# Two chained convolutions on one core: the first one split over odd and even pixels of a row, not odd and even rows

## The chip, the cores and the metric

The kernel runs on one core of a Trainium2 chip. The metric is the device time of one execution in microseconds, as the median of several executions. The five engines are called by short names below: PE (TensorE, the matrix multiplier, with PEld for its weight loads), DVE (VectorE), ACT (ScalarE), POOL (GpSimd) and SP (SyncE, which here only issues DMAs).

## What is computed

There are 8 images of 32 channels and 64 x 64 pixels, all in float32. Two blocks follow each other, each of the form "x plus a convolution of the normalised x".

```
x = x + L0(_gn(x))      # 3x3 conv, 5x5 conv, and a mix of the 5x5 result
                        # with the nine shifted 3x3 results (weights wr)
x = x + L1(_gn(x))      # for each pixel: ones and the 3x3 patch, all pairwise
                        # products of these ten, times filters (32,32,10,10)
def _gn(v, G=32, eps=1e-05):        # one group per channel: mean and variance
    m = mean over one channel's pixels; s = var over the same
    return (v - m) / sqrt(s + eps)
```

Nine shifts of a 3 x 3 convolution together with a 5 x 5 one are one 5 x 5 convolution, except at the image's border, where the shifted result was cut off. The kernel computes L0 as one 5 x 5 convolution with folded weights, plus corrections along the border.

## The kernel before

**Tiling.** Four images of 32 channels fill the 128 partitions, so there are two groups, g = 0 and 1. `raw[g]` holds x, and `plane[g]` the normalised x with a margin, at a pitch of 66 floats a row (`PITCH`). TensorE is used as 32 x 32 tiles: row group r (input partitions 32r to 32r+31) is image r, and column group s (output partitions 32s to 32s+31 of PSUM) is a "strip" s of that image. An image is worked on in two halves, h = 0 and 1 (`BANDS`). For each of them, and each image r, PSUM holds one bank `acc[:, h, r, :]` of 512 floats a partition. The upper side of the image is strips 0 and 1, the lower side strips 2 and 3, and each side gives a band of 16 rows to a half.

**Which pixels a strip is.** Before the change, of two neighbouring strips the even one holds the odd rows of the band and the odd one the even rows: 8 rows of 64 pixels, 512 outputs. A matmul with a 32 x 64 weight (two taps next to each other in y) then serves both strips from one stream of pixels, since one output row further is one tap further. `column(...)` (lines 620 to 648) walks one column of taps, `dx`, in this manner: with `pairs`, four matmuls of 32 x 64 for each image and side (`d` from -1 to 2), and without `pairs`, the two taps left over, one for each strip, as 32 x 32 matmuls on all sixteen tiles. The text calls these **pair matmuls** and **single matmuls**. Each matmul of the program is two MATMUL records in the trace. In all, the first convolution has 640 pair matmuls (1,280 records) and 320 single ones (640 records).

**Order on TensorE.** `taps0(g, h, pairs, ...)` goes over the five columns of taps in the order of `COLUMNS0`. For each group: pairs of half 0, border corrections of half 0 (`borders0`), singles of half 0, singles of half 1, border corrections of half 1, pairs of half 1. The border corrections are small matmuls: `border_row_tap` (line 655, 64 pixels of the first or last row, 20 matmuls for each g and h), `border_column_tap` (line 677, 64 pixels of the first or last column, read with a step of 66 floats, 40 for each g) and `corners` (line 665, 1 pixel). Then comes the second convolution on the same `plane`, with 13 products of shifted planes made by DVE (line 582), through the same `column`.

**Around it.** `evict` (ACT lines 327 to 334, DVE lines 542 to 549) adds nothing in the first stage and copies `acc` to `raw[g]` (a residual tap in the middle weight has already added x), image by image, three strips on ACT and strip 3 on DVE. `finish_x1` repairs borders on DVE, `statistics` and `normalise` make the next `plane[g]`. TensorE waits for a half to be evicted (`wait_evicted`) before it writes that half's banks again. There is no scheduler: every engine runs its list as written, and semaphores join them. Weights are folded on ACT and POOL (lines 363, 369, 285) and turned by a DVE transpose (line 412).

Of the kernel before, what the change touches and what calls it, by code (L numbers as in the profile page):

```python
# [5 lines left out]
B, C, H, W = 8, 32, 64, 64  # L6
GROUP = 4
NG = B // GROUP
PITCH = W + 2
# [3 lines left out]
STRIPS = 4  # L13
SIDES = 2
SIDE_ROWS = H // SIDES
BANDS = 2
BAND_ROWS = SIDE_ROWS // BANDS
CROWS = BAND_ROWS // 2
# [13 lines left out]

COLUMNS0 = (-2, -1, 1, 2, 0)
EY_EX = [(ey, ex) for ey in (-1, 0, 1) for ex in (-1, 0, 1)]
CORNERS = ((-1, -1), (-1, 1), (1, -1), (1, 1))
TAPS0 = 25
# [30 lines left out]
def conv_kernel(nc, x, w3, b3, w5, b5, wr, br, filters, out):  # L69
# [11 lines left out]
    with ctx:  # L81
# [94 lines left out]
        def product_rows(n):  # L176
            return product[n % PRODUCT_BUFS][:, PROD_AT:PROD_AT + H * PITCH]\
                .rearrange("p (y x) -> p y x", x=PITCH)[:, :, 0:W]

        def strip_rows(g, r, s, h):  # L180
# [80 lines left out]
        @block.gpsimd  # L261
        def _(pool):
            def borders_of(buf, at, length):
                nc.gpsimd.memset(buf[:, 0:at], 0.0)
                nc.gpsimd.memset(buf[:, at:at + H * PITCH].rearrange("p (y x) -> p y x", x=PITCH)[:, :, W:PITCH], 0.0)
                return nc.gpsimd.memset(buf[:, at + H * PITCH:length], 0.0)

            nc.gpsimd.memset(ones[:, :], 1.0).then_inc(zeroed, 1)
            for g in range(NG):
                borders_of(plane[g], PLANE_AT, PLANE_USED).then_inc(zeroed, 1)  # L270
            nc.gpsimd.memset(eye_from[:, :, :], 1.0).then_inc(eye_ready, 1)
            pool.wait_ge(eye_ready, 1)

            nc.gpsimd.affine_select(eye_wide[:, :, :], eye_from[:, :, :], [[-32, 4], [-1, C]], ALU.is_equal, 0.0,
                                    base=0, channel_multiplier=1).then_inc(eye_ready, 1)
            for n in range(PRODUCT_BUFS):
                borders_of(product[n], PROD_AT, PROD_USED).then_inc(borders, 1)

            pool.wait_ge(taps5_ready, 1)
            five = folded[:, 0:TAPS0, :].rearrange("p (x y) c -> p x (y c)", x=5)  # L280
            for n, (ey, ex) in enumerate(EY_EX):
                pool.wait_ge(shift_scaled, n + 1)  # L282
                three = scaled3[:, n, :, :].rearrange("p (x y) c -> p x (y c)", x=3)
                part = five[:, ex + 1:ex + 4, C * (ey + 1):C * (ey + 4)]
                nc.gpsimd.tensor_tensor(part, part, three, ALU.add).then_inc(shift_folded, 1)  # L285
                if n < len(EY_EX) - 1:
                    pool.wait_ge(shift_folded, n + 1)

        @block.scalar
        def _(act):  # L290
# [60 lines left out]
            def square(g):  # L351
# [5 lines left out]
                else:  # L357
# [2 lines left out]

            act.wait_ge(small_in, 80)
            act.wait_ge(taps5_in, 64)
            nc.scalar.activation(folded[:, 0:TAPS0, :].rearrange("p (x y) c -> p x y c", x=5),  # L363
                                 w5_in[:, :].rearrange("p (c y x) -> p x y c", y=5, x=5),
                                 ACT.Copy, scale=wr_in[:, 0:1]).then_inc(taps5_ready, 1)
            act.wait_ge(taps3_ready, 1)
            for n, (ey, ex) in enumerate(EY_EX):
# [27 lines left out]
        def _(dve):  # L395
# [6 lines left out]

            def reorder_taps():
                dve.wait_ge(small_in, 80)
                nc.vector.tensor_copy(w3_taps[:, :, :].rearrange("p (x y) c -> p x y c", x=3),  # L405
                                      w3_in[:, :].rearrange("p (c y x) -> p x y c", y=3, x=3)).then_inc(taps3_ready, 1)

            def turn_taps():

# [6 lines left out]

            def fold_edges():

                three = w3_taps[:, :, :].rearrange("p (x y) c -> p y x c", x=3)
# [117 lines left out]
            def evict(i):  # L537
# [81 lines left out]
        def _(pe):  # L619
# [29 lines left out]

            def border_row_tap(g, side, t):  # L650

                h, s, row, y = ((0, 1, 0, 0), (1, 2, CROWS - 1, H - 1))[side]
                for r in range(GROUP):
                    at = PLANE_AT + y * PITCH + t
                    nc.tensor.matmul(acc[32 * s:32 * s + 32, h, r, row * W:row * W + W],  # L655
                                     weight0[32 * r:32 * r + 32, EDGE_AT + 5 * side + t + 2, :],
                                     plane[g][32 * r:32 * r + 32, at:at + W],
                                     start=False, stop=False, tile_position=(32 * r, 32 * s))

            def corners(g, side):  # L660
                h, s, row, y = ((0, 1, 0, 0), (1, 2, CROWS - 1, H - 1))[side]
                for n, col in ((2 * side, 0), (2 * side + 1, W - 1)):
                    for r in range(GROUP):
                        at = PLANE_AT + y * PITCH + col
                        nc.tensor.matmul(acc[32 * s:32 * s + 32, h, r, row * W + col:row * W + col + 1],  # L665
                                         weight0[32 * r:32 * r + 32, CORNER_AT + n, :],
                                         plane[g][32 * r:32 * r + 32, at:at + 1],
                                         start=False, stop=False, tile_position=(32 * r, 32 * s))
# [31 lines left out]
            def wait_evicted(i):  # L700
                pe.wait_ge(evicted_act, GROUP * (i + 1))
                pe.wait_ge(evicted_dve, GROUP * (i + 1))

            def taps0(g, h, pairs, start, stop):
                for n, dx in enumerate(COLUMNS0):
                    if g == 0 and h == 0 and pairs:
                        pe.wait_ge(weight0_ready, min(n + 1, 2))
                    if dx == 0:
                        pe.wait_ge(middle_ready, g + 1)
                    five = middle0[g] if dx == 0 else weight0[:, 5 * (dx + 2):5 * (dx + 3), :]  # L710
                    last = column(h, plane[g], PLANE_AT, dx, range(-2, 3), five, start and n == 0,
                                  stop and n == len(COLUMNS0) - 1, pairs)
                return last

# [94 lines left out]
```

## Time and profile before

| | |
|---|---|
| median of 3 runs | 343.69 us (343.1 to 344.37) |
| profiled execution | 343.39 us, span 341.7 us |
| PE busy | 312.2 us, 91% of the span |
| PEld busy | 170.6 us, 50% |
| DVE busy | 180.6 us, 53% |
| ACT busy | 82.2 us, 24% |
| first MATMUL / end of the first convolution | 20.52 us / 121.3 us |

The profile is that of one execution. The span runs from its first to its last record, and the other 1.7 us of that execution's time lie around it. Records of matmuls overlap, since up to sixteen tiles work at once, so a group's mean duration is not its price: the price is read from stretches of time and the number of records in them.

### The profile page before, as it was taken

How to read it: one execution, taken by the hardware profiler on the slowest of the kernel's cores; microseconds unless marked ns; L12 is line 12 of the kernel's file. 1: busy time of each engine (PE TensorE's matmuls, PEld its weight loads, DVE VectorE, ACT ScalarE, POOL GpSimd, SP SyncE). 2: the span in 40 equal slices, each digit the busy share in tenths (PEclk: the TensorE clock that was granted, in tenths of full speed). 3: DMA queues.
4: the chain of work that ended last, by engine and by line, in shares of the span. 5: the costliest groups of instructions: out<-in, count | busy, mean ns of one | idle time of the engine just before them, and what ended most of it. 6: DMA issues, size and time to landing. Idle time of an engine off the chain costs nothing.

```text
span 341.7 us, 15524 instructions
## 1 busy us (share of the span) xinstructions
PE 312.2 (91%) x7496; PEld 170.6 (50%) x7496; DVE 180.6 (53%) x214; ACT 82.2 (24%) x135; POOL 11.3 (3%) x34
## 2 busy tenths in 40 slices
PE   0059999999999999999999999999999999999990
PEld 0023465678674445633655554744744563645550
DVE  0889628037099138205496985339003199784031
ACT  1610335052294071500000004485000000000091
POOL 3630000000000000000000000000000000000000
PEclk9999999999999999999999999999999999999998
DMA  7834100000000000000000000055000000000047
GB/s 214 279 113 107 44 4 4 2 4 3 4 4 2 4 2 3 6 2 2 4 4 2 4 4 2 17 114 125 4 2 4 2 4 2 6 2 4 4 94 154
DMA packets 7629, 11.57 MB, mean 34 GB/s; under 512 B 5392, under 2 KB 5520, under 8 KB 7440
## 3 DMA queue, kind: packets, MB, share of 16 engines
q1 hardware_dynamic: 4816, 8.54, 9.6%
q10 hardware_dynamic: 2752, 2.06, 2.2%
q8 instruction: 58, 0.95, 1.2%
q14 instruction: 3, 0.02, 0.0%
HBM read 6.40 MB, written 4.19 MB: 31 GB/s over the span
## 4 chain that ended last, share of the span: by engine, by line
PE 91%; POOL 2%; DMA 2%; issue 1%; ACTq 1%; ACT 1%; POOLq 1%; DVE 0%; DVEq 0%
PE acc L629 90%; POOL folded L285 2%; DMA w_in<-in_L_conv_w 2%; PE acc L677 1%; PE acc L655 1%; POOLq L81 1%; ACTq L236 1%; ACT folded L363 1%; DVE product L554 0%; DVEq L81 0%; PE acc L665 0%; ACTq L239 0%; ACT scaled L369 0%; DVE weight L412 0%; POOLq L282 0%
## 5 line engine op out<-in xcount | busy, mean ns | idle before, releaser
L629 PE MATMUL acc<-product,weight 32*32 32x512 f32 (+1 forms) x4416 | 182.5, 597 | 0.0
L582 DVE TENSOR_TENSOR product<-plane 128x4096 f32<-128x4096 f32 x24 | 105.1, 4424 | 63.9 <-PE acc L629 63.9
L629 PEld LDWEIGHTS acc<-product,weight 32*32 32x32 f32 (+1 forms) x4416 | 96.6, 111 | 81.8 <-issue 58.6
L629 PE MATMUL acc<-plane,weight 32*64 32x512 f32 (+1 forms) x2048 | 105.5, 603 | 21.4 <-DVE weight L412 20.5
L629 PEld LDWEIGHTS acc<-plane,weight 32*64 32x64 f32 (+1 forms) x2048 | 51.9, 121 | 65.9 <-issue 57.4
L332 ACT ACTIVATE raw<-acc,offset_by_strip 32x512 f32<-32x512 f32 x36 | 24.5, 680 | 99.5 <-PE acc L629 99.0
L629 PE MATMUL acc<-plane,middle 32*64 32x512 f32 (+1 forms) x640 | 38.2, 593 | 0.0
L330 ACT ACTIVATE raw<-acc 32x512 f32<-32x512 f32 x48 | 28.2, 588 | 36.2 <-PE acc L629 35.6
L545 DVE COPY raw<-acc 32x512 f32<-32x512 f32 x16 | 11.1, 694 | 30.9 <-PE acc L629 30.5
L629 PEld LDWEIGHTS acc<-plane,middle 32*64 32x64 f32 (+1 forms) x640 | 17.6, 119 | 12.2 <-issue 9.1
L359 ACT ACTIVATE product<-plane 128x4096 f32<-128x4096 f32 x2 | 7.3, 3636 | 63.2 <-PE acc L629 63.1
L547 DVE TENSOR_SCALAR raw<-acc,offset_by_strip 32x512 f32<-32x512 f32 x12 | 9.1, 756 | 24.0 <-PE acc L629 23.8
L500 DVE BATCH_NORM_STATS2 stats<-raw 128x6 f32<-128x512 f32 x32 | 19.5, 681 | 0.5 <-DMA raw<-in_x 0.3
L285 POOL TENSOR_TENSOR folded<-folded,scaled 128x288 f32<-128x288 f32 x9 | 8.3, 918 | 8.0 <-ACT scaled L369 7.4
L303 ACT ACTIVATE plane<-raw,norm 128x1536 f32<-128x1536 f32 x4 | 6.7, 1679 | 4.9 <-DVE norm L514 4.9
L298 ACT ACTIVATE norm<-norm 128x1 f32<-128x1 f32 x4 | 0.8, 202 | 25.5 <-DVE norm L507 25.5
L516 DVE TENSOR_SCALAR plane<-raw,mean_var,norm 128x2560 f32<-128x2560 f32 x4 | 6.8, 1712 | 0.0
L655 PE MATMUL acc<-plane,weight 32*32 32x64 f32 x160 | 5.4, 221 | 0.0
L562 DVE TENSOR_TENSOR raw<-raw,columns 128x128 f32<-128x128 f32 x2 | 0.8, 402 | 8.7 <-ACT raw L330 8.7
L655 PEld LDWEIGHTS acc<-plane,weight 32*32 32x32 f32 x160 | 4.3, 107 | 2.2 <-issue 1.8
L405 DVE COPY w_taps<-w_in 128x288 f32<-128x288 f32 x1 | 0.7, 669 | 8.8 <-DMA w_in<-in_L_conv_w 8.8
L509 DVE RECIPROCAL norm<-norm 128x1 f32<-128x1 f32 x4 | 0.7, 164 | 8.7 <-ACT norm L298 8.7
(68 smaller groups left out, 59.8 us busy)
## 6 DMA issues: line engine op xcount, KB each, us to landing
raw<-in_x SPq DMA_DIRECT2D x6, 512.0 KB, 10.2
out<-raw SPq DMA_DIRECT2D x12, 256.0 KB, 3.0
filters_in<-in_L_conv_filters SPq DMA_DIRECT2D x4, 400.0 KB, 3.9
raw<-in_x ACTq DMA_DIRECT2D x2, 512.0 KB, 8.1
out<-product SPq DMA_DIRECT2D x8, 64.0 KB, 2.4
out<-product ACTq DMA_DIRECT2D x8, 64.0 KB, 2.7
w_in<-in_L_conv_w ACTq DMA_DIRECT2D x4, 100.0 KB, 2.7
w_in<-in_L_conv_w SPq DMA_DIRECT2D x2, 36.0 KB
```

Source lines behind the costliest of these rows:

```text
L285: nc.gpsimd.tensor_tensor(part, part, three, ALU.add).then_inc(shift_folded, 1)
L303: nc.scalar.activation(inner(g, DVE_ROWS, H), raw_rows(g, DVE_ROWS, H), ACT.Identity, bias=norm[:, 6:7], scale=norm[:, 5:6]).then_inc(plan ...
L330: last = nc.scalar.activation(strip_rows(g, r, s, h), strip_acc(s, h, r), ACT.Copy)
L332: last = nc.scalar.activation(strip_rows(g, r, s, h), strip_acc(s, h, r), ACT.Identity, bias=offset_by_strip[32 * s:32 * s + 32, r, g:g + 1])
L359: nc.scalar.activation(product_rows(n), inner(g, 0, H), ACT.Square).then_inc(square_ready, 1)
L500: last = nc.vector.bn_stats(stats[:, n, :], raw[g][:, STAT * n:STAT * n + STAT])
L516: nc.vector.tensor_scalar(inner(g, 0, DVE_ROWS), raw_rows(g, 0, DVE_ROWS), mean_var[:, 0:1], norm[:, 5:6], ALU.subtract, ALU.mult).then_in ...
L545: last = nc.vector.tensor_copy(strip_rows(g, r, s, h), strip_acc(s, h, r))
L547: last = nc.vector.tensor_scalar(strip_rows(g, r, s, h), strip_acc(s, h, r), offset_by_strip[32 * s:32 * s + 32, r, g:g + 1], None, ALU.add)
L582: nc.vector.tensor_tensor(product_rows(n), inner(g, 0, H), shifted(g, PRODUCTS[k]), ALU.mult)\
L629: return nc.tensor.matmul(acc[32 * s:32 * (s + strips), h, r, :], weights[32 * r:32 * r + 32, t:t + strips, :] .rearrange("p t c -> p (t c ...
L655: nc.tensor.matmul(acc[32 * s:32 * s + 32, h, r, row * W:row * W + W], weight0[32 * r:32 * r + 32, EDGE_AT + 5 * side + t + 2, :], plane[g ...
```

## The change

The first convolution's strips become columns. Of two neighbouring strips, the even one now holds the odd pixels of each of the band's 16 rows, the odd one the even pixels: 16 rows of 32 pixels, again 512 outputs. The taps are walked row by row (`ROWS0`), and a pair of taps is two neighbours in x. A matmul's moving operand is 16 rows of 32 elements, with a step of two floats inside a row, where it was 8 rows of 64 elements with a step of one. PSUM is written as before, 512 floats in a row. The evictions of the first stage write `raw` with a step of two floats. A border row now lies on two strips, so each of its taps is two matmuls of 32 pixels. The folded weights lie in another order of taps (y outside, x inside). The second convolution, its evictions and the output stay as they are.

```diff
+        def strip_columns(g, r, s, h):
+
+            y, col = SIDE_ROWS * (s // 2) + BAND_ROWS * h, 1 - s % 2
+            return raw[g][32 * r:32 * r + 32, :].rearrange("p (y x) -> p y x", x=W)\
+                [:, y:y + BAND_ROWS, col:col + W - 1:2]
...
-            five = folded[:, 0:TAPS0, :].rearrange("p (x y) c -> p x (y c)", x=5)
+            five = folded[:, 0:TAPS0, :].rearrange("p (y x) c -> p y (x c)", y=5)
...
-                            last = nc.scalar.activation(strip_rows(g, r, s, h), strip_acc(s, h, r), ACT.Copy)
+                            last = nc.scalar.activation(strip_columns(g, r, s, h), strip_acc0(s, h, r), ACT.Copy)
...
-                            last = nc.vector.tensor_copy(strip_rows(g, r, s, h), strip_acc(s, h, r))
+                            last = nc.vector.tensor_copy(strip_columns(g, r, s, h), strip_acc0(s, h, r))
...
-                h, s, row, y = ((0, 1, 0, 0), (1, 2, CROWS - 1, H - 1))[side]
-                for r in range(GROUP):
-                    at = PLANE_AT + y * PITCH + t
-                    nc.tensor.matmul(acc[32 * s:32 * s + 32, h, r, row * W:row * W + W],
-                                     weight0[32 * r:32 * r + 32, EDGE_AT + 5 * side + t + 2, :],
-                                     plane[g][32 * r:32 * r + 32, at:at + W],
-                                     start=False, stop=False, tile_position=(32 * r, 32 * s))
+                h, half, at_row, y = ((0, 0, 0, 0), (1, 1, BAND_ROWS - 1, H - 1))[side]
+                for j in range(2):
+                    for r in range(GROUP):
+                        s = 2 * half + j
+                        at = PLANE_AT + y * PITCH + t + 1 - j
+                        nc.tensor.matmul(acc[32 * s:32 * s + 32, h, r, at_row * W // 2:(at_row + 1) * W // 2],
+                                         weight0[32 * r:32 * r + 32, EDGE_AT + 5 * side + t + 2, :],
+                                         plane[g][32 * r:32 * r + 32, at:at + W - 1:2],
+                                         start=False, stop=False, tile_position=(32 * r, 32 * s))
...
+            def tap_row(g, h, dy, weights, start, stop, pairs):
+
+
+                def tile(r, s, strips, e, t, first_one, last_one):
+                    first = PLANE_AT + (SIDE_ROWS * (s // 2) + BAND_ROWS * h + dy) * PITCH + e
+                    pixels = plane[g][32 * r:32 * r + 32, first:first + BAND_ROWS * PITCH]\
+                        .rearrange("p (y x) -> p y x", x=PITCH)[:, :, 0:W - 1:2]
+                    return nc.tensor.matmul(acc[32 * s:32 * (s + strips), h, r, :],
+                                            weights[32 * r:32 * r + 32, t:t + strips, :]
+                                            .rearrange("p t c -> p (t c)"), pixels,
+                                            start=first_one, stop=last_one, tile_position=(32 * r, 32 * s))
+
+                if pairs:
+                    for e in range(-1, 3):
+                        for s in (0, 2):
+                            for r in range(GROUP):
+                                last = tile(r, s, 2, e, e + 1, start and e == -1, stop and e == 2)
+                else:
+                    for s in range(STRIPS):
+                        for r in range(GROUP):
+                            e, t = (-2, 0) if s % 2 else (3, 4)
+                            last = tile(r, s, 1, e, t, start, stop)
+                return last
```

On TensorE, the first rows of its program before the change are these (line, operation, output and inputs, weight columns x moving elements, number of matmuls): the pairs of group 0, half 0, and its border corrections.

```order
L629 MATMUL acc<-plane,weight 64x512 x128
L629 MATMUL acc<-plane,middle_0 64x512 x32
L655 MATMUL acc<-plane,weight 32x64 x4
L677 MATMUL acc<-plane,weight 32x64 x8
L655 MATMUL acc<-plane,weight 32x64 x4
```

The same place after the change:

```order
L723 MATMUL acc<-plane,weight 64x512 x128
L723 MATMUL acc<-plane,middle_0 64x512 x32
L665 MATMUL acc<-plane,weight 32x32 x8
L689 MATMUL acc<-plane,weight 32x64 x8
L665 MATMUL acc<-plane,weight 32x32 x8
```

The large matmuls keep their number, form and place. Each group of four row taps became eight of half the length. A little further, TensorE turns from the singles of half 1 to its border corrections and its pairs. Before:

```order
L629 MATMUL acc<-plane,middle_0 32x512 x16
L655 MATMUL acc<-plane,weight 32x64 x20
L665 MATMUL acc<-plane,weight 32x1 x8
L629 MATMUL acc<-plane,weight 64x512 x128
```

After:

```order
L723 MATMUL acc<-plane,middle_0 32x512 x16
L665 MATMUL acc<-plane,weight 32x32 x40
L677 MATMUL acc<-plane,weight 32x1 x8
L723 MATMUL acc<-plane,weight 64x512 x128
```

Here the 20 row taps became 40, with nothing else between them, and nothing moved past a wait.

## Rows read from the trace of the kernel before

**Rows 1.** The page: busy time, and TensorE's granted clock in 40 slices.
```profile
PE 312.2 (91%) x7496; PEld 170.6 (50%) x7496; DVE 180.6 (53%) x214; ACT 82.2 (24%) x135; POOL 11.3 (3%) x34
...
PEclk9999999999999999999999999999999999999998
```

**Rows 2.** The chain that ended last, by line (share of the span).
```profile
PE acc L629 90%; POOL folded L285 2%; DMA w_in<-in_L_conv_w 2%; PE acc L677 1%; PE acc L655 1%; POOLq L81 1%; ACTq L236 1%; ACT folded L363 1%; DVE product L554 0%; DVEq L81 0%; PE acc L665 0%; ACTq L239 0%; ACT scaled L369 0%; DVE weight L412 0%; POOLq L282 0%
```

**Rows 3.** Waits of PE: for whom, us in total, times, longest us.
```profile
PE acc L629 <- DVE weight L412: 20.5, 1, 20.5
PE acc L629 <- issue: 0.9, 2, 0.5
```

**Rows 4.** PE by stretches: from:to, length, busy us (records), clock, DMA share, GB/s.
```profile
24.50:39.80 15.30, 15.30 (x288) 1.00 0.33 83
41.90:53.00 11.10, 10.71 (x320) 1.00 0.02 4
71.60:88.90 17.30, 17.30 (x321) 1.00 0.01 2
121.30:138.40 17.10, 17.10 (x410) 1.00 0.01 3
```

**Rows 5.** PE groups by shape: records, busy us, mean ns of one, idle before.
```profile
L629 PE MATMUL acc<-plane,weight 32*64 32x512 f32 x1280 | 73.5, 604 | 20.5 <-DVE weight L412 20.5
L655 PE MATMUL acc<-plane,weight 32*32 32x64 f32 x160 | 5.4, 221 | 0.0
L677 PE MATMUL acc<-plane,weight 32*32 32x64 f32 x160 | 4.1, 288 | 0.0
L665 PE MATMUL acc<-plane,weight 32*32 32x1 f32 x64 | 1.4, 168 | 0.0
```

**Rows 6.** The chain in order of time, 39 to 54 us: start, us, what.
```profile
39.89 0.19 PE acc L655 x4
...
41.90 1.13 PE acc L629 x20
...
53.27 0.56 PE acc L655 x35
53.83 0.13 PE acc L665 x11
```

**Rows 7.** ACT evictions of the first stage, in order of time.
```profile
48.81 7.23 ACT L330 ACTIVATE raw<-acc 32x512 f32<-32x512 f32 x12 [5.29 <-PE acc L629]
71.68 7.23 ACT L330 ACTIVATE raw<-acc 32x512 f32<-32x512 f32 x12 [15.64 <-PE acc L629]
99.45 7.21 ACT L330 ACTIVATE raw<-acc 32x512 f32<-32x512 f32 x12
121.29 7.23 ACT L330 ACTIVATE raw<-acc 32x512 f32<-32x512 f32 x12 [14.62 <-PE acc L629]
```

**Rows 8.** DVE in order of time: evictions, and the next product it waits to make.
```profile
109.15 2.86 DVE L545 COPY raw<-acc 32x512 f32<-32x512 f32 x4
121.29 2.87 DVE L545 COPY raw<-acc 32x512 f32<-32x512 f32 x4 [9.28 <-PE acc L629]
...
155.29 4.43 DVE L582 TENSOR_TENSOR product<-plane 128x4096 f32<-128x4096 f32 x1 [16.72 <-PE acc L629]
```

**Rows 9.** DVE groups by shape: border repair, columns (step 64) and rows (step 1).
```profile
L562 DVE TENSOR_TENSOR raw<-raw,columns 128x128 f32<-128x128 f32 x2 | 0.8, 402 | 8.7 <-ACT raw L330 8.7
L564 DVE TENSOR_TENSOR raw<-raw,ring_rows 128x128 f32<-128x128 f32 x2 | 0.6, 292 | 0.1
```

More of the change, by code:

```diff
@@ L31 @@
 PRODUCT_BUFS = 4
-COLUMNS0 = (-2, -1, 1, 2, 0)
+ROWS0 = (-2, -1, 1, 2, 0)
 EY_EX = [(ey, ex) for ey in (-1, 0, 1) for ex in (-1, 0, 1)]
@@ L178, in product_rows, with strip_acc0 @@
                 .rearrange("p (y x) -> p y x", x=PITCH)[:, :, 0:W]
+        def strip_columns(g, r, s, h):
+            y, col = SIDE_ROWS * (s // 2) + BAND_ROWS * h, 1 - s % 2
+            return raw[g][32 * r:32 * r + 32, :].rearrange("p (y x) -> p y x", x=W)\
+                [:, y:y + BAND_ROWS, col:col + W - 1:2]
+        def strip_acc0(s, h, r):
+            return acc[32 * s:32 * s + 32, h, r, :].rearrange("p (y x) -> p y x", x=W // 2)
         def strip_rows(g, r, s, h):
@@ L279, in _ @@
             pool.wait_ge(taps5_ready, 1)
-            five = folded[:, 0:TAPS0, :].rearrange("p (x y) c -> p x (y c)", x=5)
+            five = folded[:, 0:TAPS0, :].rearrange("p (y x) c -> p y (x c)", y=5)
             for n, (ey, ex) in enumerate(EY_EX):
                 pool.wait_ge(shift_scaled, n + 1)
-                three = scaled3[:, n, :, :].rearrange("p (x y) c -> p x (y c)", x=3)
-                part = five[:, ex + 1:ex + 4, C * (ey + 1):C * (ey + 4)]
+                three = scaled3[:, n, :, :].rearrange("p (y x) c -> p y (x c)", y=3)
+                part = five[:, ey + 1:ey + 4, C * (ex + 1):C * (ex + 4)]
                 nc.gpsimd.tensor_tensor(part, part, three, ALU.add).then_inc(shift_folded, 1)
@@ L362, in _ @@
             act.wait_ge(taps5_in, 64)
-            nc.scalar.activation(folded[:, 0:TAPS0, :].rearrange("p (x y) c -> p x y c", x=5),
-                                 w5_in[:, :].rearrange("p (c y x) -> p x y c", y=5, x=5),
+            nc.scalar.activation(folded[:, 0:TAPS0, :],
+                                 w5_in[:, :].rearrange("p (c t) -> p t c", t=25),
                                  ACT.Copy, scale=wr_in[:, 0:1]).then_inc(taps5_ready, 1)
@@ L650, in border_row_tap @@
             def border_row_tap(g, side, t):
-                h, s, row, y = ((0, 1, 0, 0), (1, 2, CROWS - 1, H - 1))[side]
-                for r in range(GROUP):
-                    at = PLANE_AT + y * PITCH + t
-                    nc.tensor.matmul(acc[32 * s:32 * s + 32, h, r, row * W:row * W + W],
-                                     weight0[32 * r:32 * r + 32, EDGE_AT + 5 * side + t + 2, :],
-                                     plane[g][32 * r:32 * r + 32, at:at + W],
-                                     start=False, stop=False, tile_position=(32 * r, 32 * s))
+                h, half, at_row, y = ((0, 0, 0, 0), (1, 1, BAND_ROWS - 1, H - 1))[side]
[7 more added lines that the diff above has]
+                                         start=False, stop=False, tile_position=(32 * r, 32 * s))
             def corners(g, side):
-                h, s, row, y = ((0, 1, 0, 0), (1, 2, CROWS - 1, H - 1))[side]
+                h, half, at_row, y = ((0, 0, 0, 0), (1, 1, BAND_ROWS - 1, H - 1))[side]
                 for n, col in ((2 * side, 0), (2 * side + 1, W - 1)):
+                    s = 2 * half + 1 - col % 2
+                    to = at_row * W // 2 + col // 2
                     for r in range(GROUP):
                         at = PLANE_AT + y * PITCH + col
-                        nc.tensor.matmul(acc[32 * s:32 * s + 32, h, r, row * W + col:row * W + col + 1],
+                        nc.tensor.matmul(acc[32 * s:32 * s + 32, h, r, to:to + 1],
                                          weight0[32 * r:32 * r + 32, CORNER_AT + n, :],
@@ L702, in wait_evicted @@
                 pe.wait_ge(evicted_dve, GROUP * (i + 1))
+            def tap_row(g, h, dy, weights, start, stop, pairs):
[18 more added lines that the diff above has]
+                return last
             def taps0(g, h, pairs, start, stop):
-                for n, dx in enumerate(COLUMNS0):
+                for n, dy in enumerate(ROWS0):
                     if g == 0 and h == 0 and pairs:
                         pe.wait_ge(weight0_ready, min(n + 1, 2))
-                    if dx == 0:
+                    if dy == 0:
                         pe.wait_ge(middle_ready, g + 1)
-                    five = middle0[g] if dx == 0 else weight0[:, 5 * (dx + 2):5 * (dx + 3), :]
-                    last = column(h, plane[g], PLANE_AT, dx, range(-2, 3), five, start and n == 0,
-                                  stop and n == len(COLUMNS0) - 1, pairs)
+                    five = middle0[g] if dy == 0 else weight0[:, 5 * (dy + 2):5 * (dy + 3), :]
+                    last = tap_row(g, h, dy, five, start and n == 0, stop and n == len(ROWS0) - 1, pairs)
                 return last
```

5 lines of the change are left out of this document (2 added, 3 removed).

## The prediction, as it was recorded before the changed kernel ran

> **What bounds the kernel now.** I read the page first. TensorE is busy for 91% of the span, at full clock in every slice but the last [rows 1]. Then the chain that ended last: 90% of it is line 629, the large matmuls of both convolutions, and the rest is mostly the start [rows 2]. Then PE's waits: it waits once for the first weights (20.5 us) and for 0.9 us besides, never for DVE, ACT or an eviction [rows 3]. So the kernel is its start plus TensorE's stream. A change in the stream's rate counts in full, a change elsewhere only if it outgrows its cover.
>
> The rate has to be read from stretches, since records overlap. A stretch of pairs has 321 records in 17.30 us [rows 4]: eight tiles (four images, two sides) run at once, so a round of 8 records takes 17.30/321 x 8 = 431 ns. A stretch of singles has 320 in 11.10 us: a round of 16 records takes 555 ns. A pair round and a single round stream as much into each tile, so the single round has some 555 - 431 = 124 ns that are not streaming. The first convolution has 1,280 pair records (160 rounds, 69 us) and 640 single ones (40 rounds, 22 us).
>
> **The change, part by part.**
>
> *The moving operand read with a step of two.* Number, length and order of the large matmuls stay. What can change is the rate of reading. The trace of before has no step of two, so I bound it from both sides. The lower bound is no cost: the output still goes to PSUM in a row and as many elements stream. The upper bound is the one stepped read there is, the border columns with a step of 66 floats [rows 5]. A 1-pixel record takes 168 ns, a 64-pixel record of neighbours 221 and of stepped pixels 288. So an element costs (221 - 168)/63 = 0.84 ns with step one and (288 - 168)/63 = 1.90 ns with step 66, that is 1.06 ns more. On 512 elements that would be 543 ns a record.
>
> Which end is nearer? Step two leaves every element's neighbour but one beside it, and every stretch of floats that is read is half used. With step 66 nothing fetched along with an element is of use. I take step two as nearer to step one, at a cost of **0**. It is the step I trust least.
>
> The Trainium skill (SBUF — State Buffer, on cachelines) says that SBUF is read in lines of 16 bytes and that two uses of a line give full bandwidth. Step two uses each line twice, so the page too would make this 0, but with nothing to spare: a row of taken pixels that starts in the second half of a line has a single use at both ends. If each such row cost one use more in 32, for half of the rows, that estimate from the page would add 1.6% to the pairs' 69 us, 1.1 us. The sum below doesn't hold it.
>
> *The border rows.* 80 matmuls of 64 pixels become 160 of 32, so 160 records are added (2 for each matmul, 40 in each of four stretches). The upper bound is today's spacing: 35 records of line 655 in 0.56 us, 16 ns each [rows 6], or 160 x 16 = 2.6 us. The lower bound is a gain: if a tile's own stream paces these stretches and not the issue, then each of its 10 records in a stretch is 32 x 0.84 = 27 ns shorter, 4 x 0.27 = 1.1 us less. Between them stands the 1-pixel row, 11 records in 0.13 us, 12 ns each [rows 6]. At 12 ns the two stretches with row taps alone go from 40 x 16 = 0.64 to 80 x 12 = 0.96 us, +0.32 each. The two that also hold column taps have 120 records between 39.89 and 41.90 us [rows 6], less 16 corner records at 12 ns, 15 ns each. There five steps of 24 records (0.36 us) would become 32 records (0.38 us), +0.1 each. I take 2 x 0.32 + 2 x 0.1 = **+0.8 us**.
>
> *The evictions.* 48 ACT and 16 DVE copies write `raw` with a step of two. Lower bound: nothing. Upper bound: DVE's repair with a step of 64 against the one with a step of one, 402 - 292 = 110 ns for 128 elements [rows 9], so 0.44 us for 512. Twelve ACT evictions of a half would take 7.23 + 5.3 = 12.5 us, DVE's four 2.87 + 1.8 = 4.6 us. Who waits? TensorE needs half 0 of group 1 emptied at 121.3 us. ACT ends it at 106.7, DVE at 112.0 [rows 7, 8], so there are 9.3 us of cover. It needs half 1 after the 384 records of half 0 of the second convolution, near 138 us (410 records lie in the 17.1 us up to 138.4 [rows 4]), and ACT ends at 128.5 us, so 10 us of cover. For group 0 the evictions end at 56.0 and 78.9 us and are needed at 71.6 and 88.9. Behind the evictions stand DVE's statistics and the next products, where DVE then idles 16.7 us [rows 8]. All cover the upper bound: **0**. If the cover were gone, each half would cost up to 5.3 us.
>
> *The weights.* Reading and folding in another order of taps keeps count, length and step of each instruction on ACT, POOL and DVE, and the first five taps are still turned first: **0** on the start of 20.5 us. The corrections' weights (line 428 and after) read with other steps, far ahead of their use at 39.8 us.
>
> The sum is made against the profiled execution, 343.39 us (span 341.7 and 1.7 around it), 0.3 below the median: 343.4 + 0 + 0.8 + 0 + 0 = 344.2 us, as a median **344.5 us**, +0.2%. This case's own range is 342.6 (borders at their gain) to 346.8 (borders at 2.6 and half a per cent on the stream).
>
> **The rivals.**
>
> *Fetches pace the stream (slower).* If a stepped read costs 1.90 ns because each element needs a fetch of its own, and a fetch with two taken elements costs the same, then step two costs 0.95 ns an element, 0.11 more than now, 56 ns a record. For it speaks that the price of a fetch, halved, is just above today's 0.84. The pairs take 160 x 56 = 9.0 us more. The singles have 124 ns a round that are not streaming, so between 0 and 2.2 us, I take 1.1. With the borders' 0.8, +10.9: **354.6 us**. It is outside 0.5% (1.7 us) from 6 ns a pair record on.
>
> *The full price of a step (slower).* Each pair record takes 543 ns more, 86.9 us. A single round goes from 555 to 431 + 543 = 974 ns, 16.8 us. With the borders: **448 us**. It needs a read that makes no use of the neighbour.
>
> *Four readers of one row group (slower).* In a single round four column groups read the same 32 partitions, in a pair round two. If the reads are shared among them and each now brings half as many useful elements, four readers at step two could be at the limit when two aren't. Then a single round takes up to 2 x 431 = 862 ns, 307 more, 40 x 307 = 12.3 us: **356.8 us**. For it: four readers at step one are the most that the trace shows. Against: nothing shows that they disturb each other now.
>
> *The gaps in the singles close (faster).* The 124 ns of a single round may come from collisions of reads: neighbouring strips now read five rows apart, and would then read the same rows, five pixels apart. If all of it goes, 40 x 124 = 5.0 us are won, **339.5 us** with the borders' 0.8. It decides from 2.5 us on, half the gaps. Against: the singles also load a weight for each record of 32 columns, twice as many in a round as the pairs, and that stays.
>
> **How the numbers follow.** The forecast has 0.44, fetches 0.27, four readers 0.09, the full price 0.07, the gaps closing 0.06, and 0.07 is for what I haven't thought of. What a measurement can tell from no change is 0.5%, 342.0 to 345.4 us. The forecast's range goes past the upper end only with the borders near their upper bound, so of its 0.44 some 0.35 are "same", 0.08 slower, 0.01 faster. Slower: 0.08 + 0.27 + 0.09 + 0.07 + 0.03 = 0.54. Faster: 0.01 + 0.06 + 0.01 = 0.08. Same: 0.38. The range takes the forecast (0.43), fetches (0.26), four readers (0.08) and a part of the rest: 342.6 to 357.2 us. It leaves out the full price and the gaps closing.
>
> **What would show it.** Pairs: the stretch of 320 records of group 1, half 0, takes 17.3 us by the forecast, 19.5 by the fetches, 39 by the full price. Singles: 320 records of group 0 take 11.1 us, by four readers up to 17.2, by closing gaps 8.6. Border stretches of half 1: near 1.0 us in place of 0.64 for the row taps. Evictions: ACT between 588 and 1,030 ns each, with no wait of PE for them. First MATMUL at 20.5 us. The prediction is wrong if step two isn't free for TensorE, and only in a small part if the borders are mis-sized.

## The result: 353.39 us, 2.8% slower

The changed kernel takes 353.39 us (median of 4 runs, 352.04 to 354.38), the kernel before 343.96 us beside it. The ratio is 1.0278, 95% interval 1.0246 to 1.0310. The profiled execution took 354.38 us, with a span of 352.6 us, 10.9 us longer than before. The medians differ by 9.4 us; the pieces below are of the two profiled executions and add up to nearly the 10.9.

The page after, with the lines that answer to [rows 1] and [rows 2]:

```profile
PE 321.0 (91%) x7656; PEld 175.6 (50%) x7656; DVE 180.8 (51%) x214; ACT 83.8 (24%) x135; POOL 11.3 (3%) x34
...
PEclk9999989999999999999999999999999999999998
...
PE acc L637 60%; PE acc L723 29%; POOL folded L294 2%; DMA w_in<-in_L_conv_w 2%; PE acc L689 1%; PE acc L665 1%; POOLq L81 1%; ACTq L245 1%; ACT folded L372 1%; DVE product L562 0%; DVEq L81 0%; PE acc L677 0%; ACTq L248 0%; ACT scaled L378 0%; DVE weight L420 0%
```

The picture is the same as before: TensorE is the chain. The 160 added records are there (7,496 became 7,656), and one slice has a lower granted clock. The waits of PE answer to [rows 3]:

```profile
PE acc L723 <- DVE weight L420: 20.7, 1, 20.7
PE acc L689 <- issue: 1.4, 1, 1.4
PE acc L677 <- issue: 1.0, 1, 1.0
PE acc L723 <- issue: 0.6, 1, 0.6
```

The start is where it was. But TensorE now stands still for 3.0 us that nothing in the profile explains ("issue"), against 0.9, and twice it does so inside the border corrections (line 689 is the column taps, 677 the corners, 665 the row taps). PE by stretches, as in [rows 4]: first singles of group 0, then its row taps of half 1, then two stretches of pairs.

```profile
45.40:58.00 12.60, 12.60 (x335) 0.86 0.01 4
58.00:59.10 1.10, 1.10 (x103) 1.00 0.00 0
59.10:77.70 18.60, 18.60 (x330) 1.00 0.01 3
77.80:96.40 18.60, 18.60 (x328) 1.00 0.01 3
```

A stretch of pairs that took 17.3 us takes 18.6 at full clock. The chain in order of time gives the best ruler, since two stretches of pairs follow each other without a break there (640 records, 80 rounds of 8). First the kernel before, then the changed one, whose other rows here are the stalls and their neighbours:

```profile
53.96 35.09 PE acc L629 x630
```

```profile
43.77 1.39 issue
...
45.42 12.59 PE acc L723 x267
58.02 1.04 PE acc L665 x53
...
59.18 37.50 PE acc L723 x604
...
100.16 0.59 issue
100.75 10.50 PE acc L723 x269
...
112.02 0.98 issue
113.25 18.89 PE acc L723 x294
132.15 33.09 PE acc L637 x714
```

A pair round went from 35.09/80 = 439 ns to 37.50/80 = 469 ns (some records are missing, the 80 rounds are the program's). Going through both chains from piece to piece, the 10.9 us lie here: four stretches of pairs +5.1 (1.5 + 2.4 + 1.2), four border stretches +3.4, singles +2.1, start +0.15. The first of the four stretches is 1.8 us longer than the last in the kernel before too (19.37 us against 17.6), which the part on the granted clock comes back to. The second convolution takes 220.4 us in both.

The evictions, as in [rows 5] and [rows 7] the group by shape and the last one in time:

```profile
L339 ACT ACTIVATE raw<-acc 32x512 f32<-32x512 f32 x48 | 30.0, 624 | 41.2 <-PE acc L723 40.5
...
L665 PE MATMUL acc<-plane,weight 32*32 32x32 f32 x320 | 6.0, 199 | 0.0
L689 PE MATMUL acc<-plane,weight 32*32 32x64 f32 x160 | 4.8, 288 | 1.4 <-issue 1.4
L677 PE MATMUL acc<-plane,weight 32*32 32x1 f32 x64 | 1.5, 172 | 1.0 <-issue 1.0
```

```profile
132.27 7.74 ACT L339 ACTIVATE raw<-acc 32x512 f32<-32x512 f32 x12 [17.23 <-PE acc L723]
```

An ACT copy went from 588 to 624 ns, and twelve from 7.23 to 7.74 us; DVE's stayed at 695 ns. No wait of PE names them.

### The profile page after: what moved, and what is told of

Same layout as the page of the kernel before. It is cut to its first block, busy times and chain, and to the rows that moved or that the text cites. A ratio compares the mean times of both kernels' runs of the same rounds, so it can differ in the third digit from the quotient of the medians.

```text
span 352.6 us, 15844 instructions
## 1 busy us (share of the span) xinstructions
PE 321.0 (91%) x7656; PEld 175.6 (50%) x7656; DVE 180.8 (51%) x214; ACT 83.8 (24%) x135; POOL 11.3 (3%) x34
## 4 chain that ended last, share of the span: by engine, by line
PE 91%; POOL 2%; DMA 2%; issue 1%; ACTq 1%; ACT 1%; POOLq 1%; DVE 0%; DVEq 0%
PE acc L637 60%; PE acc L723 29%; POOL folded L294 2%; DMA w_in<-in_L_conv_w 2%; PE acc L689 1%; PE acc L665 1%; POOLq L81 1%; ACTq L245 1%; ACT folded L372 1%; DVE product L562 0%; DVEq L81 0%; PE acc L677 0%; ACTq L248 0%; ACT scaled L378 0%; DVE weight L420 0%
## 5 line engine op out<-in xcount | busy, mean ns | idle before, releaser
L637 PEld LDWEIGHTS acc<-product,weight 32*32 32x32 f32 (+1 forms) x4416 | 98.0, 111 | 80.4 <-issue 55.6
L723 PE MATMUL acc<-plane,weight 32*64 32x512 f32 (+1 forms) x1536 | 85.5, 654 | 21.3 <-DVE weight L420 20.7
L723 PEld LDWEIGHTS acc<-plane,weight 32*64 32x64 f32 (+1 forms) x1536 | 41.8, 125 | 58.0 <-issue 55.1
L339 ACT ACTIVATE raw<-acc 32x512 f32<-32x512 f32 x48 | 30.0, 624 | 41.2 <-PE acc L723 40.5
L637 PE MATMUL acc<-plane,weight 32*64 32x512 f32 (+1 forms) x512 | 25.9, 599 | 0.0
L723 PE MATMUL acc<-plane,middle 32*64 32x512 f32 (+1 forms) x384 | 24.5, 625 | 0.0
L508 DVE BATCH_NORM_STATS2 stats<-raw 128x6 f32<-128x512 f32 x32 | 19.4, 678 | 0.1
L637 PEld LDWEIGHTS acc<-plane,weight 32*64 32x64 f32 (+1 forms) x512 | 11.6, 116 | 11.8 <-issue 9.8
L723 PEld LDWEIGHTS acc<-plane,middle 32*64 32x64 f32 (+1 forms) x384 | 11.9, 121 | 7.7 <-issue 7.0
L637 PE MATMUL acc<-plane,middle 32*64 32x512 f32 (+1 forms) x256 | 15.3, 594 | 0.0
L637 PEld LDWEIGHTS acc<-plane,middle 32*64 32x64 f32 (+1 forms) x256 | 6.5, 116 | 5.1 <-issue 3.7
L665 PEld LDWEIGHTS acc<-plane,weight 32*32 32x32 f32 x320 | 5.7, 104 | 2.3 <-issue 2.0
```

Source lines behind the costliest of these rows:

```text
L339: last = nc.scalar.activation(strip_columns(g, r, s, h), strip_acc0(s, h, r), ACT.Copy)
L508: last = nc.vector.bn_stats(stats[:, n, :], raw[g][:, STAT * n:STAT * n + STAT])
L637: return nc.tensor.matmul(acc[32 * s:32 * (s + strips), h, r, :], weights[32 * r:32 * r + 32, t:t + strips, :] .rearrange("p t c -> p (t c ...
L665: nc.tensor.matmul(acc[32 * s:32 * s + 32, h, r, at_row * W // 2:(at_row + 1) * W // 2], weight0[32 * r:32 * r + 32, EDGE_AT + 5 * side + ...
L723: return nc.tensor.matmul(acc[32 * s:32 * (s + strips), h, r, :], weights[32 * r:32 * r + 32, t:t + strips, :] .rearrange("p t c -> p (t c ...
```

## The experiments

Ratios are against the kernel before, run on the same chip. "Step" is the distance between read elements in floats.

### One part undone or done alone

**The reading undone.** In the changed kernel's `tap_row`:

```diff
-                        .rearrange("p (y x) -> p y x", x=PITCH)[:, :, 0:W - 1:2]
+                        .rearrange("p (y x) -> p y x", x=PITCH)[:, :, 0:W // 2]
```

> The changed kernel, but its large matmuls of the first convolution read 16 rows of 32 neighbouring elements in place of every other one (other pixels than the reference's, so the output differs). Theory of the step: the pairs' 18.6 us stretches go back to 17.3 and what stays is the borders' and the stalls' part, near 347.5 us in all. Rival, the form of 16 short rows and not the step: pairs stay at 18.6 us, near 353 us.

Measured: 348.56 us, ratio 1.0141 (1.0113 to 1.0169). Two stretches of pairs in the chain:

```profile
58.08 35.49 PE acc L723 x618
```

35.49 us, against 37.50 with the step and 35.09 in the kernel before. So the step costs 2.0 us of two stretches, and 16 short rows in place of 8 long ones 0.4. The form is a small part, the step the large one. The total is 1 us above what was expected for it.

**The reading alone.** In the kernel before, the large matmuls of the first convolution read what the change reads:

```diff
+                    if first_conv:
+                        first = min(first, PLANE_USED - 16 * PITCH)
+                        pixels = stack[32 * r:32 * r + 32, first:first + BAND_ROWS * PITCH]\
+                            .rearrange("p (y x) -> p y x", x=PITCH)[:, :, 0:W - 1:2]
```

> The kernel before, with nothing changed but what its large matmuls of the first convolution read: 16 rows of 32 elements with a step of two (other pixels, so the output differs). Theory of the step: the four stretches of pairs take 18.6 us in place of 17.3, 5.2 us in all, singles 0 to 1.5 us more, near 349.5 us. If the step needs the changed borders or evictions to cost something, no change from before, 344 us. If four readers of one row group hurt each other, the stretches of singles grow by several us each.

Measured: 349.96 us, ratio 1.0181 (1.0152 to 1.0210), 6.1 us more than before. The pairs again:

```profile
56.63 37.45 PE acc L633 x569
```

37.45 us, as in the changed kernel. The step needs neither the changed borders nor the evictions. Without the idle time in them, the singles of group 0 took 11.7 us against 11.0, and not several us more. Four stretches of pairs (twice 2.36 us) and the singles of two groups (1.4 us) give the 6.1.

**The added border records taken out.** In the changed kernel, `border_row_tap` issues its 20 matmuls of 64 neighbours for each half, on one strip:

```diff
-                for j in range(2):
+                for j in range(1):
                     for r in range(GROUP):
-                        s = 2 * half + j
-                        at = PLANE_AT + y * PITCH + t + 1 - j
-                        nc.tensor.matmul(acc[32 * s:32 * s + 32, h, r, at_row * W // 2:(at_row + 1) * W // 2],
+                        s = half + 1
+                        at = PLANE_AT + y * PITCH + t
+                        nc.tensor.matmul(acc[32 * s:32 * s + 32, h, r, 0:W],
...
-                                         plane[g][32 * r:32 * r + 32, at:at + W - 1:2],
+                                         plane[g][32 * r:32 * r + 32, at:at + W],
```

> The changed kernel with the border row taps in the number and form of before: 20 matmuls of 64 neighbouring elements for each half in place of 40 of 32 (on one strip alone, so the output's border rows differ). Theory: the 3.5 us that the border stretches grew, 2.0 us of them stalls with no instruction, go away, and with them the granted clock of 0.86 after the first stall: near 349.5 us. Rival, the border taps matter only by their own streaming, 0.8 us: near 352.5 us, the stalls stay.

Measured: 350.57 us, ratio 1.0201 (1.0176 to 1.0226), 2.8 us less than the changed kernel. Of PE's waits one line is left besides the start:

```profile
PE acc L723 <- issue: 0.9, 2, 0.6
```

The stalls are back at the 0.9 us of before. The expectation was 1 us too hopeful.

**The added records alone.** In the kernel before, each row tap is split into two matmuls of 32 neighbours on the same strip, and the output stays the same:

```diff
-                    nc.tensor.matmul(acc[32 * s:32 * s + 32, h, r, row * W:row * W + W],
+                    for c in (0, W // 2):
+                        nc.tensor.matmul(acc[32 * s:32 * s + 32, h, r, row * W + c:row * W + c + W // 2],
...
-                                     plane[g][32 * r:32 * r + 32, at:at + W],
+                                         plane[g][32 * r:32 * r + 32, at + c:at + c + W // 2],
```

> The kernel before with each border row tap split into two matmuls of 32 neighbouring elements, nothing else (the output stays the reference's). It has the 160 added records of the change and no stepped read. Theory: the added records cost what the changed kernel's borders and stalls did, 2.8 us by the run with wide border rows, so 346.8 us, with stalls of 1 us or more that are put down to issue in or right behind the border stretches. Rival: the stall came from the column reads or the steps, then 344.7 us at most.

Measured: 346.73 us, ratio 1.0066 (1.0050 to 1.0082), 2.5 us. The chain shows the stall in the middle of the corrections, 1.53 us long where the changed kernel has 1.39:

```profile
43.08 1.53 issue
44.92 10.41 PE acc L629 x271
55.33 1.04 PE acc L656 x54
56.57 3.59 PE acc L629 x57
```

No step is read here but the old column taps. So it is the added small matmuls that lengthen the stall, and not what they read. The row taps of half 1 (line 656) take 1.04 us, the same as line 665 after the change, and 80 records in 1.04 us are 13 ns each.

**The evictions undone.** In the changed kernel, stage 0 on ACT and DVE writes `strip_rows(g, r, s, h)` from `strip_acc(s, h, r)` again.

> The changed kernel with the first stage's evictions written as before, rows of 64 floats with a step of one (pixels go to other places, so the output differs). Theory: the evictions are covered, so ACT's copies go from 624 back to 588 ns and the time stays at 353.4 us. Rival, the writes with a step of two disturb TensorE's reads: the pairs' stretches get shorter, up to 5 us less.

Measured: 353.21 us, ratio 1.0265 (1.0227 to 1.0302). ACT's copies are back at 587 ns, the pairs take 37.41 us. The evictions' step costs nothing that can be told here and doesn't disturb TensorE's reads.

**Both costs undone.** The first and the third edit together, in the changed kernel.

> The changed kernel with both of its costs undone: the large matmuls of the first convolution read 16 rows of 32 neighbouring elements, and the border row taps have the number and form of before (other pixels and border rows than the reference's, so the output differs). What stays of the change is the 16 short rows, the evictions' step and the order of the weights. Theory: step 5.2 us and added records 2.5 to 2.8 us are all of it but some 0.2 us for each of four stretches of pairs, so 344.3 to 345.2 us. If something else in the change costs, it stays at 346 us or more.

Measured: 345.24 us, ratio 1.0033 (1.0017 to 1.0049), just above the range given. The pairs:

```profile
54.43 35.50 PE acc L723 x630
```

35.50 us is again 0.4 more than before in two stretches, 0.8 in four. That is most of the 1.2 us that are left. What the change does besides (evictions, order of the weights) has no room for a cost that can be told.

### What a stepped read costs

The next four all start from the kernel before and differ in what the first convolution's large matmuls read, in the place of the lines shown for the reading alone.

**Step four.** The rows are read as two runs of 16 elements: `[:, :, 0:W]`, then `.rearrange("p y (x j) -> p y j x", j=4)[:, :, 0:2, :]`.

> The kernel before, but the large matmuls of the first convolution read their 512 elements with a step of four floats (each of 16 rows read as two runs of 16 elements; other pixels, so the output differs). If a fetch brings four floats and costs the 1.82 to 1.9 ns of the step-66 read, each element now needs its own: 930 to 970 ns a record in place of 466 at step two, about 440 us in all. If the price is one for leaving the neighbour, whatever the step, it stays near step two, 350 us.

Measured: 435.29 us (2 runs), ratio 1.2666 (1.2622 to 1.2709). The chain's singles of group 0 (20 rounds of 16), then two stretches of pairs:

```profile
59.37 19.87 PE acc L634 x294
...
80.55 72.49 PE acc L634 x578
```

A pair round takes 72.49/80 = 906 ns, 1.77 ns an element, twice the step-two round of 468 and not the same. A single round takes 19.87/20 = 994 ns: four readers of one row group lie 88 ns above two. By the same ruler it was 110 ns before (10.98/20 = 549 against 439). So four readers don't hurt each other, even with reads at twice the price.

**Two neighbours of each four.** The rows are read as `.rearrange("p y (x j) -> p y x j", j=4)[:, :, :, 0:2]`.

> The kernel before, but the large matmuls of the first convolution read two neighbours of each four floats (elements 0, 1, 4, 5 and so on; other pixels, so the output differs). If a fetch of four floats is what costs, this uses two of each as step two does, and takes the same, 350 us. If each jump over a float costs, there are half as many jumps, near 347 us. If short runs cost, it is above 350 us.

Measured: 348.97 us, ratio 1.0156 (1.0128 to 1.0184). The pairs:

```profile
56.35 36.89 PE acc L634 x611
```

461 ns a round. This was meant to be 469 by the one theory and less by the other, and came in between; the next two runs say why.

**Rows that start at a multiple of four floats.** A row pitch of 68, and `first` rounded:

```diff
+                        first = min(first, PLANE_USED - 16 * 68 - 4) // 4 * 4
+                        pixels = stack[32 * r:32 * r + 32, first:first + 16 * 68]\
+                            .rearrange("p (y x) -> p y x", x=68)[:, :, 0:W - 1:2]
```

> The kernel before, with a step of two, and every row of 32 read elements starting at a multiple of four floats of the tensor (row pitch 68; other pixels, so the output differs). If fetches are blocks of four floats, such a row needs 16 of them and the mix in the changed kernel 16.5: record 452 ns in place of 466, near 347.5 us. If the blocks' edges don't matter, 350 us as with any start.

Measured: 348.38 us, ratio 1.0143 (1.0119 to 1.0168).

**And two floats further**, `// 4 * 4 + 2`.

> As the run that starts rows at multiples of four floats, but two floats further on (other pixels, so the output differs). If fetches are blocks of four floats, each row of 32 elements needs 17 and takes 480 ns a record, near 352.5 us. If one of the two groups' planes begins in the middle of a block, the two groups swap their roles, and the two runs take the same while their stretches differ. If edges don't matter, 350 us.

Measured: 353.57 us, ratio 1.0282 (1.0258 to 1.0306). The pairs of the one, then of the other:

```profile
55.77 36.74 PE acc L633 x605
```

```profile
57.67 38.65 PE acc L633 x623
```

459 and 483 ns a round. Two floats' shift of the start, with all else equal, is worth 5.2 us of the kernel. Both groups' stretches are alike in each run, so both planes begin on such a boundary.

|---|---|---|---|---|
| step two, start at 0 | 16 | 256 | 459 | 453 |
| step two, start at 2 | 17 | 272 | 483 | 481 |
| step two, rows alternate (the change) | 16.5 | 264 | 468 | 467 |
| two of four, a fifth of the rows start at 3 | 16.2 | 259 | 461 | 458 |
| step one, 16 rows | 8 to 9 | about 140 | 444 | 248, not the limit |

The rows alternate since the plane's pitch of 66 floats is two more than a multiple of four. "Two of four" has 17 fetches only where a row starts at the fourth float of a block, and so has fewer than step two. At step one the elements themselves are the limit, 0.84 ns each by [rows 5]. Blocks of two floats wouldn't fit: step two would then cost as much as step four.

### The border taps spread out

In the kernel before, the row taps and corners are issued one fifth at a time between the five rounds of tap columns of the same half's singles; the column taps stay. The output stays the same.

```diff
+            def rows_between(g, h, n):
+                border_row_tap(g, h, n - 2)
+                if n == 1:
+                    corners(g, h)
...
+                    if rows and h == 0:
+                        rows_between(g, h, n)
                     last = column(h, plane[g], PLANE_AT, dx, range(-2, 3), five, start and n == 0,
                                   stop and n == len(COLUMNS0) - 1, pairs)
+                    if rows and h == 1:
+                        rows_between(g, h, n)
```

> The kernel before with the row taps and the corners issued between the rounds of singles of the same half, in place of one run of them between pairs and singles (column taps stay where they are; the output stays the reference's). Theory: a round of singles has 124 ns that are not streaming, which hide 8 small records of each tile's neighbours, and instructions are used up more evenly: 2 to 3 us less than before, 341 to 342 us. Rival: singles are paced by their issue, so the added records cost their 12 to 16 ns anyway and the time stays at 344 us.

Measured: 344.28 us (12 runs), ratio 0.9991 (0.9975 to 1.0007). The theory fell. The stalls did shrink, from 0.9 us to this one row of the chain:

```profile
92.53 0.22 issue
```

But from the first border record to the next pairs group 0 takes 13.9 us (40.94 to 54.85), where it took 14.1 (39.89 to 53.96). The stalls shrank by 0.65 us in both groups together and these stretches by 0.3, so the time between the rounds isn't free for other records.

> The changed kernel with its row taps and corners issued between the rounds of singles in the same way (the output stays the reference's). Theory: with the burst gone the stalls go, 2.5 to 3.5 us less than the changed kernel, near 350 us. What stays is the price of the step. Rival: the stall depends on the number of instructions before it and not on the burst, then it only moves and the time stays near 353 us.

Measured, the same edit in the changed kernel: 352.39 us as the median of five runs, ratio 1.0239 (1.0216 to 1.0263). The interval overlaps the changed kernel's (1.0246 to 1.0310), and the hoped-for 350 us was missed. A sixth run took 357.41 us, with its first matmul only at 24.5 us. It is the profiled one, so its rows aren't used. Nothing was found that beats the kernel before.

## Why the prediction was right, and where it failed

**The range and the chances.** 342.6 to 357.2 us held the 353.39, and "slower" had the largest chance, 0.54. The likeliest single time, 344.5, was 9 us low.

**The step that failed** is "I take step two as nearer to step one, at a cost of 0". It costs the four stretches of pairs 5.1 us together with the shorter rows (30 ns x 160 rounds is 4.8), and 6.1 us of the kernel where the reading alone is changed. With the 2.5 to 2.8 us of the added records that is 8.6 to 8.9 of the measured 9.4. The reason given was that each fetched stretch is half used. It is the right picture, and the price of a fetch that stood beside it (1.90 ns, halved 0.95, against 0.84) said that half use isn't enough. The nearest row was read as a bound only, where its half was the estimate. The forecast had the mechanism wrong. The stated range held the result because a rival was given a chance.

**The rival "fetches pace the stream"** had 0.27 and said 354.6 us. It was the mechanism, shown by the steps of four and two and by the shifted start. That its total came within 1.2 us is in part luck, since two of its terms were off in opposite directions. A pair record grew by 30 ns in place of 56, because a fetch costs 1.77 ns and not 1.90, and because a round of before takes 439 ns by the chain and not the 431 that the prediction read from a window with records cut at both ends. That is 4.8 us in place of 9.0. The borders cost 2.5 to 2.8 us in place of 0.8.

The Trainium skill (SBUF — State Buffer, on cachelines) has the right block: 16 bytes, four floats. Its "≥2 hits per line for full bandwidth" does not hold here. With two uses of each line a round takes 459 ns at best, against 439 in the kernel before and 444 with the same short rows at step one. The estimate made from it, 1.1 us for rows that start in the second half, was of the right kind and order: the half of the rows with 17 fetches is worth 9 ns a round, 1.4 us.

**The borders, +0.8, were mis-sized.** The 12 ns a record was nearly right for the streaming alone: 13 ns, 1.04 us for the row taps of a half. Without idle time the four border stretches grew by 1.0 us in all. What the sum lacked is the stall. It was in the rows of before (0.9 us of "issue" [rows 3]; the chain has 0.39 and 0.48 us some 20 records behind each group's first corrections), and I took it for a constant. It grew by 2.1 us: 1.0 in the first corrections, where 120 records in a row became 160, and 1.0 in the last, where there had been none.

The stall has no releaser in the profile. The page of both kernels has a DMA queue of kind "instruction" with 16 KB packets:

```profile
q8 instruction: 60, 0.98, 1.2%
```

```profile
0.00:43.04 43.04, 22.52 (x478) 1.00 0.49 150
0.00:92.14 92.14, 71.23 (x1629) 1.00 0.24 72
```

```profile
0.00:43.78 43.78, 23.10 (x478) 1.00 0.47 147
0.00:100.16 100.16, 78.10 (x1757) 0.98 0.21 66
0.00:112.03 112.03, 89.38 (x2140) 0.98 0.19 60
```

From stall to stall it is 1,151 records before, and 1,279 and 383 after: each time one less than 9, 10 and 3 times 128 (PE's waits also take places in its list). The first stall stands behind record 478 in both, though that is a large single before the change and a column tap after it. In the kernel with split row taps the three counts are again 478, 1,757 and 2,140, and in the one with wide border rows 478 and 1,629. So TensorE stands still at the ends of 16 KB blocks of its instructions. The next end after 1,629 would be near 2,013, some 20 records into the pairs of the kernel before, and there is no stall there; after the change it falls among the corners, and there is one.

The time fits too. An instruction packet begins between 40.5 and 41.0 us before the change and between 42.5 and 43.0 after it, and TensorE goes on at 43.42 and 45.16. Counted from the first border record, it goes on after 3.5 us before and 3.6 after. The shorter records only reach the block's end sooner (2.2 us in place of 3.1) and wait there, and what stands behind it comes on top. With step four, whose large records are slower, the same block ends bring no stall, and it shrank where the taps were spread. No run changed the supply of instructions itself, but the counts leave little room for another cause.

**The granted clock.** Singles of group 0 behind the stall, after the change, then the kernel with split row taps, 44 to 50 us:

```profile
44.00:50.00 6.00, 4.84 (x117) 0.72 0.01 3
```

```profile
44.00:50.00 6.00, 5.39 (x186) 1.00 0.02 5
```

0.72 of full clock means part of the stretch at 1.2 GHz. The clock fell half a microsecond after the stall of 1.39 us and reads 0.50 from 46.0 to 49.0 us. That is 0.9 us of the +2.1 of the singles: the changed kernel's first stretch took 12.6 us, its second one 12.30 less 0.59 idle. The clock fell in the same way in the runs with the step undone (behind a stall of 1.46 us) and with the evictions undone (1.37 us). But the kernel with split row taps stood still for 1.53 us and kept its clock. So the stall alone doesn't lower it, and what does is open.

The start has a slow stretch that the clock row doesn't show. The first large records, from 20.4 to 23.5 us, first before and then after the change:

```profile
L629 PE MATMUL acc<-plane,weight 32*64 32x512 f32 x32 | 3.7, 1068 | 20.5 <-DVE weight L412 20.5
```

```profile
L723 PE MATMUL acc<-plane,weight 32*64 32x512 f32 x32 | 3.7, 1064 | 20.7 <-DVE weight L420 20.7
```

They take 1,068 and 1,064 ns, where the same records later take 590 and 621, though the clock reads 1.00 there. It is the 1,050 ns that singles take at the clock of 0.50 after the stall. It explains most of the 1.8 us by which the first stretch of pairs is longer. How long it lasts differs between executions: with the same matmuls, the first stretch took 19.4 us in the kernel before and 20.1 in the one with split row taps. While it lasts, step two and step one take the same time, so the fetches are not the limit at half speed.

**Four readers** (0.09) is refuted by step four, the **full price** (0.07) too: at step two a record grew by 30 ns and not 543, and even step four took 435 us and not 448. The **gaps** didn't close: the singles grew. The covers of the evictions held, with 36 ns of the up to 440 that I allowed, and so did the zero for the weights: the first matmul came at 20.67 us against 20.52.

## What to carry to other kernels

A float32 moving operand of TensorE is read in blocks of four floats, at 1.77 ns a block here against 0.84 ns an element. Count the blocks that each row of the operand touches, partial ones at its ends too: step one is free, step two is just past the limit, and at step four each element pays the whole block. So give rows that are read with a step of two a pitch and a start at a multiple of four floats (459 ns a round here in place of 468, still over the 444 of step one).

Small matmuls cost by their number: 13 ns for a weight load and a matmul in a long run. Where such a run holds the end of a 16 KB block of instructions, or lies just ahead of it, TensorE can stand still there, for 0.4 to 1.5 us in these runs. Splitting one in two to suit a layout has that price, even when the elements stay the same. To find such a stall, count the records up to it in two kernels.

## What the runs showed that I had not expected

A shift of the read's start by two floats changes the kernel by 5.2 us (348.38 to 353.57), with the same number of elements and instructions.

The time by which a round of singles exceeds one of pairs (124 ns in the prediction, 110 by the chain) isn't idle time to be filled: small matmuls between the rounds gained nothing that can be told (0.9991). With step four the excess is 88 ns, so it doesn't grow with the price of reading either.
